# Output stage of a two-layer cross-attention kernel: first operands loaded one stage earlier, layer-norm scaling on ScalarE, head chunks brought in one per tile

## The chip, the cores and the metric

The kernel runs on one core of a Trainium2 chip. The metric is the time of one launch in microseconds (us), lower is better. Before the change three runs gave 2204.09, 2206.16 and 2206.22 us, median 2206.16. The engines are named as the profile names them: PE is TensorE's matmul, PEld its weight load, DVE is VectorE, ACT is ScalarE, POOL is GpSimd and SP is SyncE, which here only issues DMAs. SPq is SP's instruction queue.

## The reference

2048 tokens of width 512 pass through four residual blocks. The last two are computed by the two stages that this document is about:

```python
def _layernorm(x, axis=-1, eps=1e-05):
    m = jnp.mean(x, axis=axis, keepdims=True)
    v = jnp.var(x, axis=axis, keepdims=True)
    return (x - m) / jnp.sqrt(v + eps)

# attention of layer 1, per token over its 16 heads of 32
Q, K, V = (q @ Wq.T + bq), (k @ Wk.T + bk), (v @ Wv.T + bv)      # each reshaped to 16 x 32
attn = softmax(einsum('bshd,bsgd->bshg', Q, K)) ... V
return attn @ Wo.T + bo
# feed-forward of layer 1, weights rounded to -1, 0, 1
w_ternary = jnp.clip(jnp.round(w / mean(abs(w))), -1.0, 1.0)
h = gelu(x @ w1q.T + b1);  return h @ w2q.T + b2
...
x = x + jnp.tanh(g_xattn[1]) * _L1_xattn_ref(_layernorm(x), ctx, ctx, ...)
x = x + jnp.tanh(g_ffn[1]) * _L1_ffn_ref(_layernorm(x), ...)
```

## The kernel before

The program is four stages with a barrier of all engines between them: `l0_attention` (names `a_`), `l0_experts` (`b_`), `l1_attention` (`p_`) and `l1_output_ffn` (`f_`). Each engine's program is written out by hand in order, and engines wait for each other by counting semaphores. Nothing reorders them.

Precision: a matrix product is made of a rounded part ("high") and a remainder ("low") of each operand, so every operand is first copied rounded (ACT) and then subtracted (POOL or DVE). A product of two such operands takes three matmuls (`PASSES`).

`l1_attention` works in 4 blocks of 512 tokens and 8 pairs of units per block (`p` from 0 to 31). Beside it SP brings 32 pieces of the feed-forward weights into the two buffers `w_piece`, and ACT (L1917) and DVE (L2162) sum their magnitudes, one piece each per `p` from `p` = 20 on. A buffer is loaded again (`load_piece`, L1715) when its piece is summed. At the end of each block the heads are stored to `aT` in DRAM (`store_heads`, L1720). The tensor `carry` (16 x 512 per partition) serves as space for weights, queries and context there.

`l1_output_ffn` has two parts. The output part goes over 16 tiles of 128 tokens:

- SP loads the heads as chunks of 128 rows x 512 tokens, four per block of tokens (L2332, ring of 4), the output weights `woT` as four chunks (L2344, two buffers), the bias `bo`, the tokens `x2` (L2346, L2352) and the pieces of the feed-forward weights (L2337).
- ACT rounds each head chunk (L2409) and weight chunk (L2414). POOL makes the low parts of the heads (L2376), DVE those of `woT` (L2519).
- For tile n PE makes the product (`project_out`, L2449, 12 matmuls). DVE adds it to the tokens (L2541) after POOL has added the bias (L2381), takes the statistics (L2544, L2546, L2548), POOL raises variance + eps to the power -0.5 (L2390), and DVE normalises (L2555). PE turns the tile (`turn`, L2458, 4 transposes), ACT rounds the turned tile (L2417) and DVE makes its low part (L2561).
- PE's order is `project_out(n)`, `turn(n - 2)`. DVE's order is add and statistics of n, low part of n - 2, normalise n. ACT rounds two head chunks behind each turned tile for n = 0 to 5, and POOL makes two low parts behind each power (`chunks_beside`).
- Before its first tile DVE rounds two pieces of the feed-forward weights (L2512, L2514).

The second part is the feed-forward over 4 blocks of 512 tokens: `hidden` (L2476, 32 matmuls per group), Gelu on ACT, `down` (L2490, 32 matmuls per group), 4 groups per block. The first `hidden` stands behind the last `turn` on PE.

Of the kernel before, what the change touches and what calls it, by code (L numbers as in the profile page):

```python
# [22 lines left out]
BLK = 512  # L23
# [1453 lines left out]
def l1_attention(nc, new_sem, x_shared, expert_out, place, weight, carry, ctxT, W, w_ffn, x2, qT, kT, vT, aT, sums):  # L1477
# [41 lines left out]
    with ExitStack() as c:  # L1519
# [697 lines left out]
def l1_output_ffn(nc, new_sem, x2, aT, W, w_ffn, sums, out):  # L2217
# [16 lines left out]
    with ExitStack() as c:  # L2234
# [15 lines left out]
        y = sb("y", [P, NT, D])  # L2250
# [29 lines left out]
        w_rounded = sem("w_rounded")  # L2280
        const_in = sem("const_in")
# [3 lines left out]
        x_in = [sem(f"x_in{n}") for n in range(NBLK)]  # L2285
        wo_in = [sem(f"wo_in{s}") for s in range(2)]
# [10 lines left out]
        ln_eps = sem("ln_eps")  # L2297
        ln_rstd = sem("ln_rstd")
# [16 lines left out]
        wo_t = W["woT"].rearrange("(k p) (c n) -> k c p n", p=P, n=BLK)  # L2315
# [372 lines left out]
```

## Time and profile before

| | |
|---|---|
| timed runs, median (range) | 2206.16 us (2204.09 to 2206.22) |
| the profiled execution | 2200.77 us |
| its span, first to last instruction | 2199.0 us |
| PE busy | 1969.6 us, 90% |
| DVE, ACT, POOL busy | 1017.7, 826.7, 1094.9 us |
| mean granted TensorE clock | 0.943 |
| `l1_attention`'s last head copy on ACT ends | 1835.6 us |
| first instruction of `l1_output_ffn` | 1842.4 us |
| first matmul of the feed-forward | 1950.2 us |
| last instruction | 2199.0 us |

The span is read as four stages one behind the other. The output part stands between 1842.4 and 1950.2 us; the rest of the stage is the feed-forward. All times in the rows below are microseconds from the span's start.

### The profile page before, as it was taken

To read this page: it belongs to the slowest core of one execution; us is meant where nothing else is said; L and a number is where in the kernel's file an instruction comes from. 1 tells how busy PE (TensorE), PEld (TensorE's weight loads), DVE (VectorE), ACT (ScalarE), POOL (GpSimd) and SP (SyncE) were. 2 spreads that over 40 slices of the span, in tenths; PEclk is the share of its full clock that TensorE was granted. 3 is DMA by queue.
4 is the path that set the end of the run, shared out by engine and by line. 5 is a ranking of instruction groups with operands and counts; after the bars stand their busy time and mean duration, and the time that the engine had idled before them with its cause. 6 is when DMAs were issued, how large, how long until landed. Compare 5 with 4: busy or idle time off the path is not lost. (4 is left out here: it accounts for less than half of the span.)

```text
span 2199.0 us, 30241 instructions
## 1 busy us (share of the span) xinstructions
PE 1969.6 (90%) x10428; PEld 1649.3 (75%) x10428; DVE 1017.7 (46%) x1561; ACT 826.7 (38%) x1578; POOL 1094.9 (50%) x805
## 2 busy tenths in 40 slices
PE   6999999999999999689996999985799874789998
PEld 5888788878887888478884899983677653568886
DVE  3556654755476547623331333335466343583111
ACT  3336332633363336231211222223377763233332
POOL 6755576557655774441147646606254222533332
PEclk9999999999999999879998999997899966899999
DMA  4232323133313331362326655427676635222000
GB/s 155 82 105 68 116 96 106 53 108 116 107 48 112 101 124 30 118 214 82 139 95 204 197 164 161 131 75 210 175 187 153 169 113 184 81 68 67 19 19 19
DMA packets 173869, 251.29 MB, mean 114 GB/s; under 512 B 45040, under 2 KB 69616, under 8 KB 173744
## 3 DMA queue, kind: packets, MB, share of 16 engines
q1 hardware_dynamic: 158656, 205.23, 30.0%
q0 software_dynamic: 9472, 34.09, 4.9%
q10 hardware_dynamic: 5616, 10.23, 1.2%
q8 instruction: 88, 1.44, 0.3%
q14 instruction: 37, 0.30, 0.0%
HBM read 182.92 MB, written 66.58 MB: 113 GB/s over the span
## 5 line engine op out<-in xcount | busy, mean ns | idle before, releaser
L238 POOL TENSOR_TENSOR a_w_hl<-a_w_raw,a_w_hl 128x2048 fp32r<-128x2048 f32 x65 | 299.8, 4613 | 164.6 <-ACT a_w_hl L300 164.4
L413 PE MATMUL a_proj<-a_c_hl,a_w_hl 128*128 128x512 f32 x768 | 183.2, 399 | 21.4 <-DVE a_w_hl L530 19.6
L300 ACT ACTIVATE a_w_hl<-a_w_raw 128x2048 fp32r<-128x2048 f32 x66 | 126.2, 1912 | 164.6 <-PE a_proj L413 106.7
L413 PEld LDWEIGHTS a_proj<-a_c_hl,a_w_hl 128*128 128x128 f32 x768 | 146.2, 192 | 53.8 <-issue 19.6
L487 PE MATMUL a_proj<-a_w_hl,a_a_hl 128*128 128x512 f32 x768 | 179.5, 392 | 4.0 <-DVE a_a_hl L586 4.0
L413 PE MATMUL a_proj<-a_w_hl,a_c_hl 128*128 128x512 f32 x768 | 181.3, 392 | 0.0
L413 PE MATMUL a_proj<-a_a_hl,a_w_hl 128*128 128x512 f32 x768 | 176.4, 390 | 0.0
L319 ACT ACTIVATE a_sq<-a_proj,a_vecs 128x512 f32<-128x512 f32 x128 | 87.9, 689 | 228.6 <-PE a_proj L413 149.1
L487 PEld LDWEIGHTS a_proj<-a_w_hl,a_a_hl 128*128 128x128 f32 x768 | 142.7, 188 | 34.3 <-POOL a_w_hl L238 5.5
L413 PEld LDWEIGHTS a_proj<-a_a_hl,a_w_hl 128*128 128x128 f32 x768 | 143.6, 188 | 29.7
L262 POOL TENSOR_TENSOR a_ssum<-a_ssum,a_sq 128x512 f32<-128x512 f32 x112 | 145.6, 1300 | 36.9 <-ACT a_sq L319 33.2
L413 PEld LDWEIGHTS a_proj<-a_w_hl,a_c_hl 128*128 128x128 f32 x768 | 142.4, 188 | 28.7
L1252 PE MATMUL b_gate_up<-b_wts,b_xt_hl 128*128 x936 | 159.4, 326 | 4.2 <-DVE b_xt_hl L1451 4.2
L1252 PEld LDWEIGHTS b_gate_up<-b_wts,b_xt_hl 128*128 128x128 f32 x936 | 154.5, 190 | 8.2 <-issue 5.0
L2398 POOL TENSOR_TENSOR f_a_hl<-f_act_sb,f_a_hl 128x512 fp32r<-128x512 f32 x64 | 86.0, 1345 | 149.0 <-ACT f_a_hl L2430 148.9
L1160 PE MATMUL b_gate_up<-b_wts 128*128 128x512 f32 (+1 forms) x576 | 142.0, 407 | 3.0 <-POOL b_wts L937 2.5
L586 DVE SCALAR_TENSOR_TENSOR a_a_hl<-a_qT,a_vecs,a_a_hl 128x512 fp32r<-128x512 f32 x64 | 105.1, 1672 | 83.4 <-ACT a_a_hl L333 83.4
L1160 PEld LDWEIGHTS b_gate_up<-b_wts 128*128 128x128 f32 (+1 forms) x576 | 106.8, 186 | 34.3 <-POOL b_wts L937 2.6
L2490 PE MATMUL f_totals<-f_ternary,f_a_hl 128*128 128x512 f32 x512 | 122.5, 396 | 0.0
L2476 PE MATMUL f_hidden<-f_h_hl,f_ternary 128*128 x512 | 121.0, 394 | 0.0
L1829 POOL TENSOR_TENSOR p_probs<-p_probs,p_rden 128x512 f32<-128x512 f32 x64 | 68.0, 1068 | 99.6 <-DVE p_rden L2158 99.1
L1924 ACT ACTIVATE p_probs<-p_probs,p_mx 128x128 f32<-128x128 f32 x256 | 99.1, 390 | 47.5 <-DVE p_mx L2154 47.4
(245 smaller groups left out, 3682.5 us busy)
## 6 DMA issues: line engine op xcount, KB each, us to landing
a_w_raw<-in_a_ki_w SPq DMA_DIRECT2D x18, 1024.0 KB, 5.2
a_w_raw<-in_a_vi_w SPq DMA_DIRECT2D x16, 1024.0 KB, 5.1
a_w_raw<-in_a_q_w SPq DMA_DIRECT2D x16, 1024.0 KB, 5.1
a_w_raw<-in_a_o_w SPq DMA_DIRECT2D x16, 1024.0 KB, 5.4
b_gu_raw<-in_b_gate_up POOLq DMA_DIRECT2D x32, 352.0 KB, 3.7
l_sorted_rows<-b_zeros SPq DMA_DIRECT2D x39, 256.0 KB, 3.3
b_hs<-l_sorted_rows SPq DMA_DIRECT2D x39, 256.0 KB, 3.2
l_expert_out<-b_yg ACTq DMA_DIRECT2D x39, 256.0 KB, 3.5
```

The costliest lines, as they stand in the source:

```text
L238: pool.tensor_tensor(w_hl[:, s, 1], w_raw[:, s], f32(w_hl[:, s, 0]), ALU.subtract)\
L262: pool.tensor_tensor(ssum[:], first, sq[:, n % 2, :], ALU.add).then_inc(sq_added, 1)
L300: act.activation(w_hl[:, i % 2, 0], w_raw[:, i % 2], ACT.Copy).then_inc(w_high, 1)
L319: act.activation(sq[:, n % 2, :], proj[:, j, :], ACT.Square, bias=bias)\
L413: mm = pe.matmul(proj[:, j, :], left, right, start=(k == 0 and n == 0), stop=(k == KC - 1 and n == 2))
L487: mm = pe.matmul(proj[:, j, :], a_hl[:, ap, k, j * P:(j + 1) * P], w_hl[:, i % 2, wp, k], start=(n == 0 and m == 0), stop=(n == 4 * G - 1 ...
L586: dve.scalar_tensor_tensor(a_hl[:, 1, n % 4, :], qT[:, n, :], v_b[:, n:n + 1], f32(a_hl[:, 0, n % 4, :]), ALU.add, ALU.subtract).then_inc( ...
L1160: mm = pe.matmul(gu_ps[0:w, n, part, :], gu_hl[:, s, wp, k, cols], h_hl[:, hslot, ap, k, :], start=(k == 0 and m == 0), stop=(k == KC - 1 ...
L1252: mm = pe.matmul(gu_ps[:, i % 2, half, 0:F], x_part(i, xp)[:, own], part(r, P, at, F), start=(k == 0 and xp == 0 and start == HI), stop=(k ...
L1924: e = act.activation(probs[:, r, y, :], probs[:, r, y, :], ACT.Exp, bias=mx[:, r, y:y + 1], accum_out=den[:, r, y:y + 1])
L2476: mm = pe.matmul(h_ps[:, m % 2, :], w_t[:, 2 * g, k, f * P:(f + 1) * P], h_hl[:, ap, k, bass.ds(BLK * t, BLK)], start=(k == 0 and ap == 0) ...
L2490: mm = pe.matmul(y_ps[:, j, :], a_hl[:, ap, f, j * P:(j + 1) * P], w_t[:, 2 * g + 1, f, :], start=(m == 0 and ap == 0), stop=(m == NG * FC ...
```

## The change

In `l1_attention`, at `p` = 28, SP issues twelve more loads, of 256 KB each, into `carry`: the four head chunks of the first block of tokens, the four chunks of `woT`, and the first four tiles of tokens. `l1_output_ffn` gets `carry` and uses it as its tile buffer `y`, so these operands lie in place when the stage begins. The tokens of blocks 1 and 3 are loaded where `woT` and the first heads lay, as soon as those are taken.

In the output part, ACT normalises in place of DVE: `Identity` with scale = rstd and bias = -mean x rstd. DVE makes -mean (`neg`), POOL the product (`shift`). Chunks 4 to 7 of the heads are rounded and split before the first tile's power, and from then on one chunk per tile, for n = 0 to 7. The first two pieces of feed-forward weights are rounded by DVE beside tiles 8 and 10, with `act_sb` as their spare buffer, and `tg_b2` is scaled behind the last piece.

```diff
 (l1_attention, SP, in the loop over p)
+                if n == NBLK and w == 4:
+                    sp.wait_ge(c_split, KC * NBLK)
+                    sp.wait_ge(o_out, 16 * NQ)
+                    for k in range(KC):
+                        sp.dma_start(y_next[:, 3 * TPB + k, :], heads_t[k][0]).then_inc(next_in, 16)
+                    sp.wait_ge(s_ready, NP * (NBLK - 1))
+                    for k in range(KC):
+                        sp.dma_start(y_next[:, TPB + k, :], wo_t[k]).then_inc(next_in, 16)
+                    sp.wait_ge(q_moved, NBLK)
+                    for j in range(TPB):
+                        sp.wait_ge(x2_out[j], 16 * NBLK)
+                        sp.dma_start(y_next[:, j, :], x2[j * P:(j + 1) * P, :]).then_inc(next_in, 16)
 (l1_output_ffn)
-        y = sb("y", [P, NT, D])
+        y = carry.rearrange("p (n d) -> p n d", d=D)
+        wo_raw, first_raw = y[:, TPB:2 * TPB, :], y[:, 3 * TPB:4 * TPB, :]
-        def chunks_beside(n):
-            return range(KC + 2 * n, min(KC * NBLK, KC + 2 * n + 2))
+        AHEAD = 2 * KC
+        def chunk_beside(n):
+            return [AHEAD + n] if AHEAD + n < KC * NBLK else []
+        ROUNDED = (8, 10)
 (SP)
-            for k in range(KC):
-                load_chunk(k)
-                if k >= 2:
-                    sp.wait_ge(wo_split, k - 1)
-                sp.dma_start(act_sb[:, k % 2, :], wo_t[k][0]).then_inc(wo_in[k % 2], 16)
-            sp.dma_start(tg_bo[:], W["bo"].to_broadcast([P, D])).then_inc(const_in, 16)
-            sp.dma_start(y[:, 0:TPB, :], x2_t[0]).then_inc(x_in[0], 16)
+            sp.dma_start(tg_bo[:], W["bo"].to_broadcast([P, D])).then_inc(bo_in, 16)
+            for n in range(KC, AHEAD):
+                load_chunk(n)
+            sp.dma_start(y[:, 2 * TPB:3 * TPB, :], x2_t[2]).then_inc(x_in[2], 16)
+            sp.wait_ge(wo_split, KC)
+            sp.dma_start(y[:, TPB:2 * TPB, :], x2_t[1]).then_inc(x_in[1], 16)
+            sp.wait_ge(a_split, KC)
+            sp.dma_start(y[:, 3 * TPB:4 * TPB, :], x2_t[3]).then_inc(x_in[3], 16)
+            for n in range(AHEAD, KC * NBLK):
+                load_chunk(n)
             for m in range(2):
                 load_piece(m)
...
 (POOL)
-            pool.wait_ge(const_done, 2)
+            pool.wait_ge(const_done, 1)
             add_bias(0)
             add_bias(1)
-            for n in range(NT):
-                pool.wait_ge(ln_eps, n + 1)
-                pool.tensor_tensor(rstd[:, n % 2, :], rstd[:, n % 2, :], mhalf[:], ALU.pow).then_inc(ln_rstd, 1)
+            for n in range(KC, AHEAD):
+                a_low(n)
+            for n in range(NT + 2):
+                if n < NT:
+                    pool.wait_ge(ln_eps, 2 * n + 2)
+                    pool.tensor_tensor(rstd[:, n % 2, :], rstd[:, n % 2, :], mhalf[:], ALU.pow).then_inc(ln_pow, 1)
+                    pool.wait_ge(ln_pow, n + 1)
+                    pool.tensor_tensor(shift[:, n % 2, :], neg[:, n % 2, :], rstd[:, n % 2, :], ALU.mult)\
+                        .then_inc(ln_rstd, 1)
                 if n + 2 < NT:
                     add_bias(n + 2)
 (ACT)
+            def normalise(n):
+                s = n % 2
+                act.wait_ge(ln_rstd, n + 1)
+                if n >= 2:
+                    act.wait_ge(h_turned, n - 1)
+                act.activation(hs[:, s, :], y[:, n, :], ACT.Identity, bias=shift[:, s, :], scale=rstd[:, s, :])\
+                    .then_inc(ln_done, 1)
+            for n in range(NT + 2):
+                if n >= 2:
+                    h_high_part(n - 2)
+                if n < NT:
+                    normalise(n)
+                for m in chunk_beside(n):
+                    a_high_part(m)
 (DVE)
-            round_piece(0)
-            round_piece(1)
...
+                if n >= 2:
+                    dve.wait_ge(ln_done, n - 1)
+                dve.tensor_scalar(neg[:, s, :], mv[:, s, 0:1], -1.0, None, ALU.mult).then_inc(ln_eps, 1)
                 dve.tensor_scalar(rstd[:, s, :], mv[:, s, 1:2], LN_EPS, None, ALU.add).then_inc(ln_eps, 1)
...
                 if n >= 2:
                     h_low_part(n - 2)
-                if n < NT:
-                    normalise(n)
+                if n in ROUNDED:
+                    round_piece(ROUNDED.index(n), 0)
```

PE's program is as before. Three places show how the instructions move. The first is SP at the end of `l1_attention` (heads stored to `l_aT`, weight pieces, then the next stage), before:

```order
L1715 DMA p_w_piece<-in_w_ffn 128x512 x12
L1720 DMA l_aT<-p_o 32x16x128 x4
L1715 DMA p_w_piece<-in_w_ffn 128x512 x8
L1720 DMA l_aT<-p_o 32x16x128 x4
L1519 UNCONDITIONAL_BRANCH
L2325 UNCONDITIONAL_BRANCH
L2327 DMA f_gates<-in_d_gates 128x2
```

and after:

```order
L1719 DMA p_w_piece<-in_w_ffn 128x512 x12
L1724 DMA l_aT<-p_o 32x16x128 x4
L1719 DMA p_w_piece<-in_w_ffn 128x512 x2
L1783 DMA carry<-l_aT 128x512 x4
L1786 DMA carry<-in_d_woT 128x512 x4
L1790 DMA carry<-x 128x512 x4
L1719 DMA p_w_piece<-in_w_ffn 128x512 x6
L1724 DMA l_aT<-p_o 32x16x128 x4
L1519 UNCONDITIONAL_BRANCH
L2353 UNCONDITIONAL_BRANCH
L2355 DMA f_gates<-in_d_gates 128x2
```

The twelve loads into `carry` stand between the second and the third of the last eight pieces. The second place is POOL at the start of the output part and over its first tiles (`f_h_hl` is a low part of a head chunk, `f_y` or `carry` the bias added to a tile), before:

```order
L2376 TENSOR_TENSOR f_h_hl<-f_a_raw,f_h_hl 128x512 x4
L2381 TENSOR_TENSOR f_y<-f_y,f_tg_bo 128x512 x2
L2390 TENSOR_TENSOR f_rstd<-f_rstd,f_mhalf 128x1
L2381 TENSOR_TENSOR f_y<-f_y,f_tg_bo 128x512
L2376 TENSOR_TENSOR f_h_hl<-f_a_raw,f_h_hl 128x512 x2
L2390 TENSOR_TENSOR f_rstd<-f_rstd,f_mhalf 128x1
L2381 TENSOR_TENSOR f_y<-f_y,f_tg_bo 128x512
```

and after:

```order
L2403 TENSOR_TENSOR f_h_hl<-carry,f_h_hl 128x512 x4
L2409 TENSOR_TENSOR carry<-carry,f_tg_bo 128x512 x2
L2403 TENSOR_TENSOR f_h_hl<-f_a_raw,f_h_hl 128x512 x4
L2421 TENSOR_TENSOR f_rstd<-f_rstd,f_mhalf 128x1
L2423 TENSOR_TENSOR f_shift<-f_neg,f_rstd 128x1
L2409 TENSOR_TENSOR carry<-carry,f_tg_bo 128x512
L2403 TENSOR_TENSOR f_h_hl<-f_a_raw,f_h_hl 128x512
L2421 TENSOR_TENSOR f_rstd<-f_rstd,f_mhalf 128x1
L2423 TENSOR_TENSOR f_shift<-f_neg,f_rstd 128x1
L2409 TENSOR_TENSOR carry<-carry,f_tg_bo 128x512
L2403 TENSOR_TENSOR f_h_hl<-f_a_raw,f_h_hl 128x512
```

Four more low parts stand ahead of the first power, and each tile then holds power, shift, one bias and one low part. The third place is ACT from the last chunk of weights on (`f_totals` is a turned tile, `f_hs` a normalised one), before:

```order
L2414 ACTIVATE f_a_hl<-f_act_sb 128x512
L2409 ACTIVATE f_h_hl<-f_a_raw 128x512
L2414 ACTIVATE f_a_hl<-f_act_sb 128x512
L2417 ACTIVATE f_h_hl<-f_totals 128x4x128
L2409 ACTIVATE f_h_hl<-f_a_raw 128x512 x2
L2417 ACTIVATE f_h_hl<-f_totals 128x4x128
L2409 ACTIVATE f_h_hl<-f_a_raw 128x512 x2
```

and after:

```order
L2446 ACTIVATE f_a_hl<-carry 128x512
L2461 ACTIVATE f_tgs<-f_gates 128x2
L2442 ACTIVATE f_h_hl<-f_a_raw 128x512 x4
L2452 ACTIVATE f_hs<-carry,f_shift,f_rstd 128x512
L2442 ACTIVATE f_h_hl<-f_a_raw 128x512
L2452 ACTIVATE f_hs<-carry,f_shift,f_rstd 128x512
L2442 ACTIVATE f_h_hl<-f_a_raw 128x512
L2457 ACTIVATE f_h_hl<-f_totals 128x4x128
L2452 ACTIVATE f_hs<-carry,f_shift,f_rstd 128x512
L2442 ACTIVATE f_h_hl<-f_a_raw 128x512
L2457 ACTIVATE f_h_hl<-f_totals 128x4x128
```

The normalising of tile n stands between the copy of the turned tile n - 2 and one chunk.

## Rows read from the trace of the kernel before

**Rows 1.** Chain of waits, start of the stage: start us, us, what.
```profile
1842.80 0.42 SPq L2332
...
1844.21 4.33 DMA f_act_sb<-in_d_woT
...
1852.18 8.40 DMA f_w_raw<-in_w_ffn
...
1865.94 1.27 POOL f_y L2381
```
**Rows 2.** Chain of waits, one tile with two chunks.
```profile
1904.59 2.52 POOL f_h_hl L2376 x2
1907.11 0.52 POOL f_rstd L2390
...
1907.66 1.48 DVE f_hs L2555
...
1909.18 0.67 PE f_totals L2458 x4
```
**Rows 3.** Timeline, a tile without chunks: start us, us, engine, line [idle before <-releaser].
```profile
1923.46 0.74 DVE L2541 SCALAR_TENSOR_TENSOR f_y<-f_totals,f_tgs,f_y 128x512 f32<-128x512 f32 x1
...
1925.18 0.15 DVE L2548 TENSOR_SCALAR f_rstd<-f_mv 128x1 f32<-128x1 f32 x1
1925.25 0.68 DVE L2561 TENSOR_TENSOR f_h_hl<-f_totals,f_h_hl 128x512 fp32r<-128x512 f32 x1
...
1926.00 1.51 DVE L2555 TENSOR_SCALAR f_hs<-f_y,f_mv,f_rstd 128x512 f32<-128x512 f32 x1
```
**Rows 4.** Timeline, first turn, last projection, a late normalising, first feed-forward matmuls.
```profile
1873.15 0.60 PE L2458 MATMUL f_totals<-f_ident,f_hs 128*128 128x128 f32 x4
...
1940.22 3.05 PE L2449 MATMUL f_totals<-f_a_hl,f_h_hl 128*128 128x512 f32 x12
...
1945.84 0.55 DVE L2555 TENSOR_SCALAR f_hs<-f_y,f_mv,f_rstd 128x512 f32<-128x512 f32 x1
...
1950.21 6.04 PE L2476 MATMUL f_hidden<-f_h_hl,f_ternary 128*128 x16
```
**Rows 5.** Timeline, POOL's first low parts.
```profile
1847.33 4.63 POOL L2376 TENSOR_TENSOR f_h_hl<-f_a_raw,f_h_hl 128x512 fp32r<-128x512 f32 x3
```
**Rows 6.** Timeline, an Identity with a bias on ACT.
```profile
1700.37 0.68 ACT L1888 ACTIVATE p_outs<-p_proj,p_bias 128x512 f32<-128x512 f32 x1
```
**Rows 7.** Timeline, a short DVE operation beside two long ones of POOL.
```profile
1497.51 3.00 POOL L1823 TENSOR_TENSOR p_w_hl<-carry,p_w_hl 128x512 fp32r<-128x512 f32 x2
...
1499.07 0.15 DVE L2112 TENSOR_SCALAR p_rstd<-p_mv 128x1 f32<-128x1 f32 x1
```
**Rows 8.** Chain of waits, one group of the feed-forward.
```profile
1967.39 7.25 PE f_hidden L2476 x32
```
**Rows 9.** Timeline, a weight piece rounded alone and one beside POOL.
```profile
1952.48 0.75 DVE L2512 TENSOR_SCALAR f_hs<-f_w_raw,f_thr 128x1024 f32<-128x1024 f32 x1 [0.57 <-DVE f_h_hl L2561]
1953.27 1.28 DVE L2514 SCALAR_TENSOR_TENSOR f_ternary<-f_w_raw,f_thr,f_hs 128x1024 fp32r<-128x1024 f32 x1
...
1988.11 1.60 DVE L2512 TENSOR_SCALAR f_hs<-f_w_raw,f_thr 128x1024 f32<-128x1024 f32 x1
1989.74 2.20 DVE L2514 SCALAR_TENSOR_TENSOR f_ternary<-f_w_raw,f_thr,f_hs 128x1024 fp32r<-128x1024 f32 x1
```
**Rows 10.** Timeline, end of `l1_attention`: SP's pieces and DVE's sums.
```profile
1805.07 21.81 SPq L1715 DMA_DIRECT2D p_w_piece<-in_w_ffn  x8
...
1815.75 0.66 DVE L2162 TENSOR_REDUCE magnitudes<-p_w_piece 128x1 f32<-128x512 f32 x1
...
1819.37 0.69 DVE L2150 TENSOR_TENSOR p_probs<-p_scores,p_mask 128x512 f32<-128x512 f32 x1 [2.96 <-PE p_scores L2043]
```
**Rows 11.** Stretches: us, PE, PEld, DVE, ACT, POOL busy, PEclk, DMA share, GB/s.
```profile
1848.00:1855.00 7.00, 4.94 (x9) 2.50 (x9) 3.87 (x4) 3.68 (x6) 5.03 (x4) 0.50 0.72 203
1855.00:1868.00 13.00, 5.30 (x15) 3.92 (x15) 6.75 (x11) 0.00 (x0) 2.25 (x3) 0.76 1.00 368
```

More of the change, by code:

```diff
@@ L1473, in _, with l1_attention @@
                     take_tile(i - 2)
-def l1_attention(nc, new_sem, x_shared, expert_out, place, weight, carry, ctxT, W, w_ffn, x2, qT, kT, vT, aT, sums):
+def l1_attention(nc, new_sem, x_shared, expert_out, place, weight, carry, ctxT, W, w_ffn, woT, x2, qT, kT, vT, aT, sums):
     T, D = x2.shape
@@ L1609, in l1_attention @@
         o_out = sem("o_out")
+        next_in = sem("next_in")
+        y_next = carry.rearrange("p (n d) -> p n d", d=D)
+        heads_t = aT.rearrange("(k p) (b t) -> k b p t", p=P, t=BLK)
+        wo_t = woT.rearrange("(k p) n -> k p n", p=P)
         x_t, x2_t = (a.rearrange("(b n p) d -> n b p d", p=P, n=TPB) for a in (x_shared, x2))
@@ L2214, in _, with l1_output_ffn @@
             reciprocal(2 * NP * NBLK - 1)
-def l1_output_ffn(nc, new_sem, x2, aT, W, w_ffn, sums, out):
+def l1_output_ffn(nc, new_sem, x2, aT, W, w_ffn, sums, carry, out):
     T, D = x2.shape
@@ L2270, in l1_output_ffn @@
         rstd = sb("rstd", [P, 2, 1])
-        w_neg = hs[:].rearrange("p s d -> p (s d)")
+        neg = sb("neg", [P, 2, 1])
+        shift = sb("shift", [P, 2, 1])
+        w_neg = {0: act_sb[:].rearrange("p s d -> p (s d)"), 1: hs[:].rearrange("p s d -> p (s d)")}
         gates_in = sem("gates_in")
@@ L2284, in l1_output_ffn @@
         const_done = sem("const_done")
-        x_in = [sem(f"x_in{n}") for n in range(NBLK)]
-        wo_in = [sem(f"wo_in{s}") for s in range(2)]
+        x_in = {n: sem(f"x_in{n}") for n in range(1, NBLK)}
         wo_high = sem("wo_high")
@@ L2297, in l1_output_ffn @@
         ln_eps = sem("ln_eps")
+        ln_pow = sem("ln_pow")
         ln_rstd = sem("ln_rstd")
@@ L2418, in _ @@
                                y_ps[:, 2 + n % 2, :].rearrange("p (k n) -> p k n", k=KC), ACT.Copy).then_inc(h_high, 1)
-                for m in chunks_beside(n):
+            act.wait_ge(gates_in, 16)
+            act.activation(tgs[:], gates[:], ACT.Tanh).then_inc(tg_ready, 1)
+            for n in range(KC, AHEAD):
+                a_high_part(n)
+            for n in range(NT + 2):
[3 more added lines that the diff above has]
+                    normalise(n)
+                for m in chunk_beside(n):
                     a_high_part(m)
-            act.wait_ge(const_in, 48)
+            act.wait_ge(const_in, 32)
             with act.Fori(0, NBLK) as t:
@@ L2629, in build @@
                 stage(l1_attention, x_shared, expert_out, place, weight, carry[:], a["ctxT"], part("c_"), a["w_ffn"],
-                      x2, qT, kT, vT, aT, sums)
-            stage(l1_output_ffn, x2, aT, part("d_"), a["w_ffn"], sums, out)
+                      a["d_woT"], x2, qT, kT, vT, aT, sums)
+                stage(l1_output_ffn, x2, aT, part("d_"), a["w_ffn"], sums, carry[:], out)
     last[0].close()
```

59 lines of the change are left out of this document (25 added, 34 removed).

## The prediction

> **What bounds the kernel now.** I read the chain of waits first, from its end back. The feed-forward is PE without a gap, one group of 32 matmuls after the other in 7.25 us [rows 8], from the first `hidden` matmul at 1950.21 us on. So everything that the change can bring is an earlier start of that matmul; the work behind it keeps its order, and I take it as unchanged.
>
> The part before it splits in three on the chain. At the start the chain is loads and their users: a weight chunk takes 4.33 us from issue to landing, then the stage waits 8.40 us for a weight piece, because DVE rounds two pieces before it scales the bias, and POOL adds the first bias only at 1865.94 [rows 1]. PE turns tile 0 at 1873.15 [rows 4]. In the tiles with two chunks the chain goes through POOL and DVE: two low parts 2.52, power 0.52, normalising 1.48, turn 0.67, from 1904.59 to 1909.85 [rows 2], and then ACT's copy of the turned tile and of the next chunk, 0.6 each, before POOL can go on: 6.5 us per tile. In the tiles without chunks DVE is full: from the add at 1923.46 to the end of the normalising at 1927.5 (1926.00 + 1.51) it does one tile in 4.0 us, of which normalising takes 1.51 [rows 3]. The same instruction takes 0.55 where POOL adds no bias beside it [rows 4].
>
> **The change, part by part.** All times are on the clock of the profiled execution (2200.77 us, span 2199.0).
>
> *Start up to the first turn.* The heads, `woT` and tokens lie in place. ACT needs 8 copies of some 0.65 us [rows 6], from 1842.4 to about 1847.6, so it is early. POOL starts no earlier than before: its first low part began at 1847.33 [rows 5], behind its own constants and the clearing of semaphores, which stays. From there POOL is the queue: four low parts at 1.3 (between 1.26 [rows 2] and 1.54, that is 4.63 / 3 [rows 5]) to 1852.6, two biases at 1.27 [rows 1] to 1855.2, four low parts at 1.26 to 1860.2, power 0.55 to 1860.8. The new product `shift` is not in the trace. It is a POOL operation on 128x1 like the power, so at most 0.57; it can't be less than nothing; I take 0.5 and 0.1 for the wait between the two, to 1861.4. The normalising on ACT: an Identity with a bias on 128x512 took 0.68 [rows 6]; I take 0.7, with 0.5 and 1.0 as ends, to 1862.1. PE has done tiles 0 to 2 by then, at the low clock at first (granted 0.50, which is 1.2 GHz, in 1848 to 1855, behind a wait of 12 us) [rows 11]. First turn: 1862.1 instead of 1873.15, 11 us saved. The tokens' loads go with it at no cost: they are asked for by POOL's second tile at the earliest.
>
> *Tiles with a chunk (n = 0 to 7).* Per tile POOL does power 0.52, shift 0.6, bias 1.27, low part 1.26 = 3.65 us. The chunk's copy stands on ACT behind the normalising: shift ends at 1.1, normalising at 1.85, copy at 2.5, low part at 3.75. I take 3.75 per tile, the cover being nearly gone: every 0.1 us more on ACT's normalising is 0.1 more per tile. Turn 8 then comes at 1862.1 + 8 x 3.75 = 1892.1.
>
> *What PE can do.* Its tile is 12 matmuls and 4 transposes. In the feed-forward, where nothing is waited for, a matmul of this width takes 7.25 / 32 = 0.227 us [rows 8], so 12 take 2.72, plus about 0.45 for the turn: 3.17. The bound on the other side is the 3.05 that 12 matmuls show alone [rows 4] plus the turn's 0.67 and a gap, 3.8. I take 3.2, since `project_out(n)` waits only for the add of n - 2 and the turn for a tile two behind. DVE without the normalising: 1923.46 to 1925.93 is 2.47, plus 0.08 for `neg`, 2.6 [rows 3].
>
> *Tiles 8 to 15.* Four more turns at 3.2 bring 1904.9, then project 15 starts 0.45 later and takes 3.05: 1908.4. Beside them DVE rounds two pieces. One takes 0.75 + 1.28 alone and 1.60 + 2.20 beside POOL [rows 9]; at 3 us each, DVE has 4 x 2.6 + 6 = 16.4 us for four tiles in which PE has 12.8, and the two-tile lead on PE gives back most of it. I put 1.5 on the path (0 to 4). Project 15 ends at 1909.9 instead of 1943.27 (1940.22 + 3.05).
>
> *Tail.* Before, DVE lagged and 6.94 us passed from 1943.27 to 1950.21. Now: add, statistics, mean and variance 2.0 (1923.46 to 1925.33, plus `neg` and a semaphore), power 0.6, shift 0.6, normalising 0.75, turn 0.75 = 4.7. The feed-forward starts at 1914.6, 35.6 us earlier.
>
> *The twelve loads in `l1_attention`.* SP sends them between 1806 and 1812 (0.47 us each with the gap [rows 1]), where it had been idle till ACT's next sum, so the issue is covered. Their 3.1 MB are not: DMA moved 368 GB/s at full share, and 203 at 0.72 share with chunks, that is 280 [rows 11]. So they drain in 8.5 to 11 us, to 1817 or 1819, and the two pieces behind them land at 1818 to 1820.5. DVE sums one at 1815.75 and then has 2.96 us of idle time up to 1819.37 [rows 10]. The stall is 0 to 2 us; I take 1.5, and 5 as the outer end, if the next pair is late as well. The Trainium skill ("DMA: Bandwidth & Descriptors", Queues, rings and completion order) says that the DMAs of one issuing engine run on one row of rings and are consumed in ring order. By that rule the pieces can't overtake the loads, as I have assumed from the 8.40 us of a 512 KB piece behind a 1 MB load; if they could, this term would be 0.
>
> *Edits at nothing.* `tg_b2` scaled behind the last piece (DVE is done with the pieces long before the first `down` ends), the waits on `next_in` (landed by 1820, asked for at 1842), one more semaphore. ACT's switch between Copy, Identity and Tanh: in `l1_attention` Identity stands between Exps and copies with no table load in the rows, and the program has one load in this stage, before Gelu, as before.
>
> **The sum.** 35.6 - 1.5 = 34.1 us. Profiled execution 2200.77 - 34.1 = 2166.7. The timed median was 2206.16, 5.4 above the profiled one, so the forecast is 2172 us timed.
>
> **A rule that speaks against it.** `neg` and `rstd` are single-source operations on DVE and now fall beside POOL's long operations. In the trace a 128x1 operation of that kind took 0.15 us in the middle of two POOL operations that lasted 3.00 [rows 7], while the 128x512 one took 1.51 against 0.55 [rows 3, 4]. The Trainium skill ("GPSIMD Engine Reference", Key points) says that GpSimd shares its SBUF interfaces with VectorE and contends with its instructions in a two-port mode or with two SBUF inputs. The normalising agrees with it; read strictly it would hold the two short ones as well, which rows 7 doesn't show. By the rule so read, the time would be that of rival 1.
>
> **The rivals.**
> 1. *The short operations on DVE wait out POOL's.* Two of them per tile at up to 1.27 each: DVE 2.6 + 2.5 = 5.1 per tile. Turn 13 at 1862.1 + 13 x 5.1 = 1928.4, feed-forward at about 1935: saved 15 - 1.5 = 13.5, timed 2192.5. For: the normalising did so. Against: rows 7. Chance 0.04.
> 2. *The start isn't shortened*, because a first copy or POOL's low parts are held by something that the loads had hidden so far (ACT's first instruction, the bias landing late). Price up to 11 us: timed 2183. For: SP's first chunk load leaves at 1842.80 [rows 1], and no row shows what ACT and POOL do when nothing is awaited from it. Against: nothing that the first copies need is loaded in the stage any more. Chance 0.06.
> 3. *POOL or ACT is slower per tile than reckoned and PE takes 3.8*: normalising 1.0 on ACT, or stretched low parts. 4.1 x 8 for the first tiles (2.8 more), 0.6 x 4 for the others (2.4), rounding hidden in it (-1.5): some 4 to 5 us, timed 2176. It lies in the range. Chance 0.14.
> 4. *Slower than before: the tiles run in lockstep.* ACT's order puts the copy of turned tile n - 2 ahead of normalising n, and DVE's waits on `ln_done` stand ahead of its low part; if one of them closes a loop over one tile, its length is project 3.05 + DVE 2.0 + power and shift 1.2 + normalising 0.7 + turn 0.7 + copy 0.6 + low part 0.7 = 8.9 us. Turn 15 would be at 1862.1 + 15 x 8.9 = 1995.6, 46 us behind the old one: timed some 2253. It becomes slower than before from 5.8 us per tile ((1949.4 - 1862.1) / 15). For: every buffer is only two deep. Against: with the same depths the old kernel ran at 4.0 [rows 3], and the loop that I find (turn, copy, normalising) is 2 us long over two tiles. Chance 0.02.
> That the change doesn't do what it says, for example that the loads land in `carry` too late, is excluded by 20 us between their landing and the barrier.
>
> **How the numbers follow.** Forecast 0.74, rival 1 0.04, rival 2 0.06, rival 3 0.14, rival 4 0.02. The forecast's own ends: rounding and stall both hidden, 3 us better, 2169, and shift, normalising and DMA cheaper, 2166; on the other side the stall at 5 and the rounding at 4 make 2178. With rival 3 and the reach towards rival 2 the range is 2163 to 2184. A difference under 0.2% (4.4 us) can't be told from no change. Only rival 4 is slower: faster 0.97, same 0.01, slower 0.02.
>
> **What would show it.** First turn near 1862 and first low part of POOL still near 1847.4 (plus the stall); turns 3.7 to 3.8 apart up to turn 8, with POOL or ACT's normalising named as what ended PE's waits; about 3.2 apart behind that, with DVE named at tiles 9 to 12; 4.7 us from the last projection to the first `hidden`; the first DVE sum behind the twelve loads 2 to 5 us late and the last head copy 0 to 2 us late; the granted clock at 1.00 from turn 0 on. The forecast is wrong if turns stay over 4.5 apart, if `neg` takes over 0.5 us, or if the feed-forward itself becomes longer than 2199.0 - 1950.2 = 248.8 us by more than 1.

## The result and the profile after

The changed kernel took 2168.32 us (median of four, 2160.28 to 2171.64) against 2205.12 us for the kernel before beside it. The ratio is 0.9837, 95% interval 0.9806 to 0.9867. The forecast was 2172 us. A second comparison, beside the last experiments, gave 2167.29 us and 0.9834 (0.9811 to 0.9857). The profiled execution took 2160.28 us with a span of 2158.5.

| from the stage's first instruction | before | after | forecast |
|---|---|---|---|
| first turn of a tile | 30.75 | 19.45 | 19.7 |
| turn 8 | 81.20 | 48.70 | 49.7 |
| last projection ends | 100.87 | 66.04 | 67.5 |
| first `hidden` | 107.81 | 70.45 | 72.2 |
| first `down` | 117.33 | 78.33 | |
| last instruction | 356.60 | 317.67 | 321.0 |

The stage begins at 1842.40 us before and at 1840.83 after.

The chain of waits through the first tile and one steady tile of the changed kernel (start us, us, what; POOLq is POOL's sequencer, L2662 clears a semaphore):

```profile
1840.85 0.04 POOLq L2662
...
1845.23 0.20 POOL f_ones L2392
...
1845.97 5.13 POOL f_h_hl L2403 x4
1851.10 2.50 POOL carry L2409 x2
1853.60 4.98 POOL f_h_hl L2403 x4
1858.58 0.54 POOL f_rstd L2421
...
1859.19 0.20 POOL f_shift L2423
...
1859.41 0.81 ACT f_hs L2452
...
1866.21 0.20 POOL f_shift L2423
...
1867.15 0.62 ACT f_h_hl L2442
...
1867.85 1.29 POOL f_h_hl L2403
1869.13 0.52 POOL f_rstd L2421
```

No DMA stands on it any more [rows 1 had two]. For 4.4 us the chain is POOL clearing semaphores, and from 1845.97 on 12.6 us of POOL's low parts and biases without a gap, then power, shift and ACT's normalising. The steady tile is the loop that the prediction described: shift 1866.21, normalising 0.81, the chunk's copy 1867.15, low part 1867.85, power 1869.13, and the next shift 3.51 us behind the first. In [rows 2] it was 6.5. PE is behind this loop at first: turn 1 comes 4.85 us behind turn 0. Turns 1 to 6 are then 3.23 to 3.27 us apart, and at turn 7 PE has caught up with the loop. So turn 7 stands 24.6 us behind turn 0, seven times 3.51.

The timeline around tiles 8 and 10, where a weight piece is rounded:

```profile
1886.45 0.80 DVE L2562 TENSOR_SCALAR f_act_sb<-f_w_raw,f_thr 128x1024 f32<-128x1024 f32 x1
1886.66 1.00 POOL L2421 TENSOR_TENSOR f_rstd<-f_rstd,f_mhalf 128x1 f32<-128x1 f32 x1
1887.29 1.28 DVE L2564 SCALAR_TENSOR_TENSOR f_ternary<-f_w_raw,f_thr,f_act_sb 128x1024 fp32r<-128x1024 f32 x1
1887.74 0.88 POOL L2423 TENSOR_TENSOR f_shift<-f_neg,f_rstd 128x1 f32<-128x1 f32 x1
...
1888.66 0.81 ACT L2452 ACTIVATE f_hs<-carry,f_shift,f_rstd 128x512 f32<-128x512 f32 x1 [2.84 <-POOL f_shift L2423]
...
1889.53 0.66 PE L2508 MATMUL f_totals<-f_ident,f_hs 128*128 128x128 f32 x4 [1.20 <-ACT f_hs L2452]
...
1897.33 3.05 PE L2499 MATMUL f_totals<-f_a_hl,f_h_hl 128*128 128x512 f32 x12 [0.65 <-DVE carry L2587]
```

At tile 8 DVE isn't late. POOL is: its power takes 1.00 us instead of 0.55 and its shift 0.88 instead of 0.20, both beside a rounding operation, and PE waits 1.20 us for the normalising behind them. Behind tile 10 PE waits 0.65 us for DVE itself (its add of tile 11), and turn 11 comes 0.9 us late.

The timeline of the tail, and DVE behind it:

```profile
1906.98 0.75 DVE L2587 SCALAR_TENSOR_TENSOR carry<-f_totals,f_tgs,carry 128x512 f32<-128x512 f32 x1 [0.66 <-PE f_totals L2499]
...
1909.01 0.55 POOL L2421 TENSOR_TENSOR f_rstd<-f_rstd,f_mhalf 128x1 f32<-128x1 f32 x1 [2.39 <-DVE f_rstd L2597]
...
1910.72 0.66 PE L2508 MATMUL f_totals<-f_ident,f_hs 128*128 128x128 f32 x4 [2.55 <-ACT f_hs L2452]
...
1911.28 7.53 PE L2526 MATMUL f_hidden<-f_h_hl,f_ternary 128*128 x32
...
1919.16 2.13 PE L2540 MATMUL f_totals<-f_ternary,f_a_hl 128*128 128x512 f32 x8 [0.35 <-DVE f_ternary L2564]
```

The last add starts as soon as the last projection ends, so DVE has no arrears. From the last projection's end to the first `hidden` it is 4.4 us, where it was 6.94 before [rows 4]. And the timeline at the end of `l1_attention`, which answers to [rows 10]:

```profile
1806.34 2.34 SPq L1790 DMA_DIRECT2D carry<-x  x4
...
1808.72 8.58 SPq L1719 DMA_DIRECT2D p_w_piece<-in_w_ffn  x4
...
1813.70 1.21 PE L2060 MATMUL p_scores<-p_k,carry 32*128 32x128 f32 x16
1815.67 0.63 ACT L1934 ACTIVATE p_w_piece<-p_w_piece 128x512 f32<-128x512 f32 x1 [1.94 <-DMA p_w_piece<-in_w_ffn]
...
1816.26 0.69 DVE L2179 TENSOR_REDUCE magnitudes<-p_w_piece 128x1 f32<-128x512 f32 x1 [4.82 <-DMA p_w_piece<-in_w_ffn]
1816.87 0.68 DVE L2167 TENSOR_TENSOR p_probs<-p_scores,p_mask 128x512 f32<-128x512 f32 x1
...
1822.42 2.08 PE L2060 MATMUL p_scores<-p_k,carry 32*128 32x128 f32 x16
```

Both sums wait for pieces issued from 1808.72 on, behind the twelve loads. The twelve have landed by 1815.0 and the two pieces at 1815.65 and 1816.24. That is 6.9 and 7.0 us behind their issue, and the next pair needs 2.8. DVE's masking stands behind its sum, and the score groups, 6.83 to 6.88 us apart just ahead of this, are 8.72 apart here. Behind this gap PE's next score group takes 2.08 us instead of 1.21, at a lower clock (granted 0.50 from 1817.3 to 1830.9). From the fourth last score group to the next stage it is 40.78 us, and 38.00 before: the stall costs 2.8 us, once.

### The profile page after: what moved, and what is told of

Its sections match the earlier page's. It is cut to its first block and busy times, and to the rows that moved or that the text cites. A ratio compares the mean times of both kernels' runs of the same rounds, so it can differ in the third digit from the quotient of the medians.

```text
span 2158.5 us, 30291 instructions
## 1 busy us (share of the span) xinstructions
PE 1953.0 (90%) x10428; PEld 1641.9 (76%) x10428; DVE 998.5 (46%) x1561; ACT 837.7 (39%) x1594; POOL 1099.1 (51%) x821
```

## The experiments

In twelve runs the stage of the output began anywhere from 1836.1 to 1849.6 us of the span, with the same code ahead of it but for the loads. `l1_attention` itself began at 1478.5 to 1488.9. That spread is larger than most effects looked for, so I read each variant from its trace, by spans inside the stage, and give the timed ratio beside it. "Attention's end" is the time from the fourth last score group to the first instruction of the output stage.

| | attention's end | first turn | first `hidden` | stage | timed, ratio to before |
|---|---|---|---|---|---|
| before | 38.00 | 30.75 | 107.81 | 356.60 | |
| after | 40.78 | 19.45 | 70.45 | 317.67 | 0.9837 |
| x9 after again | 40.73 | 19.44 | 70.49 | 317.69 | 0.9834 |
| x1 loads late | 37.99 | 23.12 | 76.20 | 324.30 | 0.9876 |
| x2 rounding first | 40.60 | 23.05 | 71.93 | 320.14 | 0.9863 |
| x3 DVE normalises | 40.36 | 21.06 | 83.36 | 331.21 | 0.9904 |
| x4 two chunks | 40.24 | 17.18 | 73.74 | 321.37 | 0.9861 |
| x5 before, ACT normalises | 37.98 | 30.96 | 84.73 | 333.04 | 0.9879 |
| x6 loads spread | 37.97 | 19.43 | 70.41 | 318.59 | 0.9817 |
| x7 copy first | 40.30 | 19.89 | 68.52 | 316.70 | 0.9821 |
| x8 start as before | 38.01 | 29.17 | 78.16 | 326.92 | 0.9853 |
| x10 start balanced | 37.99 | 19.84 | 68.32 | 316.42 | 0.9822 |
| x11 spread and copy | 37.97 | 19.75 | 68.76 | 316.59 | 0.9823 |
| x12 behind the pieces | 40.71 | 19.47 | 70.49 | 317.69 | one run |

The first column has two values and nothing between: 37.97 to 38.01 without the burst of twelve loads, 40.24 to 40.78 with it.

### x3 and x5: what the normalising on ScalarE is worth

```diff
 x3, the changed kernel
-                if n < NT:
-                    normalise(n)        (ACT)
+                if n < NT:
+                    normalise(n)        (DVE, behind h_low_part; no neg, no shift)
```

> The changed kernel, but DVE normalises as before; no neg and no shift. Theory A (DVE becomes the bound): 3.9 us per tile instead of 3.5 and 3.25, the rounding of two pieces fully on the path (+4), tail +2: 13 to 17 us slower than the changed kernel, about 2182. Theory B (PE and POOL bound the tiles, the move of the normalising is worth little): 3 us slower.

Measured: first `hidden` 12.9 us later, stage 13.5 us longer, 2180.30 us, ratio 0.9904 (0.9872 to 0.9936). Theory A holds in size and place: the turns are 3.97 us apart, and the tail takes 6.94 us instead of 4.4. DVE in x3, one tile:

```profile
1882.78 1.51 DVE L2588 TENSOR_SCALAR f_hs<-carry,f_mv,f_rstd 128x512 f32<-128x512 f32 x1
1884.21 0.74 DVE L2574 SCALAR_TENSOR_TENSOR carry<-f_totals,f_tgs,carry 128x512 f32<-128x512 f32 x1
...
1886.75 1.51 DVE L2588 TENSOR_SCALAR f_hs<-carry,f_mv,f_rstd 128x512 f32<-128x512 f32 x1
```

The period is 3.97 us and DVE is never idle in it.

```diff
 x5, the kernel before
+ DVE:  neg = -mean;  POOL: shift = neg * rstd behind the power
+ ACT:  h_high_part(n - 2), normalise(n), chunks_beside(n)
- DVE:  normalise(n)
```

> The kernel before, with one part of the change alone: ScalarE normalises, with neg on DVE and shift on POOL. Loads, chunks and rounding as before. Theory A (DVE's normalising set the period in both kinds of tile; with two chunks POOL then takes the 4.8 us that x4_two_chunks showed): first turn still at 30.7 us behind the stage's start, 1.7 us less for each of some 6 tiles, 0.75 less for 8, 4 less at the tail: 17 to 21 us faster than before, some 2185. Theory B (the parts add up, so this one is worth what its undoing cost, 13.5 us): 2190.

Measured: 2179.38 us, ratio 0.9879 (0.9849 to 0.9909); first `hidden` at 84.73 instead of 107.81, so 23.1 us earlier from this part alone. Both theories were too small. Between turns 2 and 6 they are 4.06 us apart on average (6.5 before); only two intervals reach the 4.8 of POOL's loop with two chunks, in the others PE uses up the lead that POOL had. And 6.0 us are won ahead of turn 2 (47.28 before, 41.25 in x5), which I had not counted at all. So this part is worth 23.1 us when it is added first (x5) and 12.9 when it is taken away last (x3): what a part is worth depends on which others stand.

### x1, x2 and x8: what the start is made of

```diff
 x1: no loads into carry in l1_attention; in the output stage
+            for k in range(KC):
+                sp.dma_start(first_raw[:, k, :], a_t[k][0]).then_inc(op_in[2 * k], 16)
+                sp.dma_start(wo_raw[:, k, :], wo_t[k]).then_inc(op_in[2 * k + 1], 16)
 x2: in DVE's program ahead of tg_bo (SP loads both pieces behind bo)
+            round_piece(0, 0)
+            round_piece(1, 0)
 x8: both
```

> The changed kernel, but the twelve operands are loaded at the start of the output stage (heads and weights by turns, then bias and tokens), none in the attention stage. Theory A (POOL and DVE's rounding set the old start, the loads only a part): POOL starts its low parts about 5 us behind the stage's start as now, the biases wait for the tokens to 14.5 to 17.5, the second four low parts follow, first turn at 22 to 27 us instead of 19.45; the stall of 1.9 us in the attention stage goes. Net 1 to 5 us slower than the changed kernel, 2169 to 2174 timed. Theory B (the loads a stage ahead carry the 11 us of the start): first turn at 30 us, 9 us slower, about 2177.

> The changed kernel, but the first two weight pieces are rounded ahead of tile 0 as before the change (SP loads them behind the output bias), and tg_bo is scaled behind them. Theory A (either the rounding or the late loads alone would have held the start, so one of them costs little): rounding lies beside POOL's first four low parts, bias from 11.2 us behind the stage's start instead of 10.2, and the 1.20 and 0.65 us that PE waits beside tiles 8 and 10 go; within 2 us of the changed kernel. Theory B (moving the rounding is what shortened the start): 6 us or more slower.

> The changed kernel with both changes of the start undone: operands loaded in the output stage, and two weight pieces rounded ahead of tile 0. Either alone gave the first turn at 23.1 us behind the stage's start (19.45 with neither). Theory A (they stand one behind the other: the pieces queue behind the operands and the biases behind the rounding): first turn at 30 to 33 us, so 7 to 10 more than either alone. Theory B (they overlap): 24 to 26 us.

Measured: first turn at 23.1 us with either undone, at 29.2 with both, and at 19.45 with neither. In x1 POOL's bias waits 2.60 us for the tokens, in x2 2.35 us for DVE behind the rounding, in x8:

```profile
1855.96 0.75 DVE L2557 TENSOR_SCALAR f_act_sb<-f_w_raw,f_thr 128x1024 f32<-128x1024 f32 x1 [2.81 <-DMA f_w_raw<-in_w_ffn]
...
1860.14 0.48 DVE L2577 TENSOR_SCALAR f_tg_bo<-f_tg_bo,f_tgs 128x512 f32<-128x512 f32 x1
```

So of the 9.7 us at the start the part made first wins 6.1 and the second 3.6, whichever is which. In x1 the first turn lies in theory A's 22 to 27. The first `hidden` is 5.8 us late, 2.1 of them behind the first turn: turns 1 to 7 are all 3.52 apart, at the pace of POOL's loop, where PE in the changed kernel caught up with it. Less the 2.8 us of the stall that x1 avoids, and with a slower first `hidden` group, the trace is 3.8 us worse than that of the changed kernel, within theory A's 1 to 5; the timed median, 2174.27, lies 0.3 outside its range. x2 holds to theory A in the total and not at the start: its first turn is 3.6 us late, and the first `hidden` only 1.5, since nothing waits beside tiles 8 and 10. From the first turn on x2 is 2.1 us faster than the changed kernel, which is what the rounding costs there. x8's first turn is just outside theory A's 30 to 33.

### x4: one chunk per tile or two

```diff
-            return [AHEAD + n] if AHEAD + n < KC * NBLK else []
+            return list(range(KC + 2 * n, min(KC * NBLK, KC + 2 * n + 2)))
```

> The changed kernel, but no chunks ahead of the first power and two per tile beside tiles 0 to 5, as before the change. Theory A (POOL has to make the same low parts either way, and PE has its three projections done only at 17 us): turns from 17.2 us on, 4.9 us apart for six tiles, turn 8 at 51 to 53 us instead of 48.7: 2 to 4.5 us slower. Theory B (the period of the old tiles, 6.5 us, comes from the two chunks): 3 us per tile, 18 us slower.

Measured: first turn 17.18, first `hidden` 3.3 us later, ratio 0.9861 (0.9825 to 0.9897). Theory A holds in the total (2 to 4.5 us) and less well in the turns. POOL's powers are 4.7 to 4.8 us apart, as it said, but the turns are that far apart only twice. Between turns 1 and 2 it is 7.34 us: `project_out(4)` waits 2.43 us for POOL's low part and then takes 4.46 us, at a granted clock of 0.64. Turn 8 comes at 50.7, just ahead of theory A's 51 to 53. From x5 (two chunks, old start) to x8 (one chunk, old start) it is 6.6 us, so this part too is worth more in the other order.

### x6 and x12: the stall in `l1_attention`

```diff
 x12: the block of twelve loads, word for word, moved from ahead of
      load_piece to behind it in the same pair of units
 x6:  the same place, four loads at w == 4, four at w == 5, four at w == 6
```

> The changed kernel, with the twelve early loads spread over three pairs of units, four behind the weight pieces of each, in place of all twelve between two pieces. Theory A (the stall is pieces queued behind 3.1 MB of loads): all intervals between score groups 6.8 to 6.9 us, 0.9 to 1.9 us gained ahead of the output stage, the output stage as in the changed kernel. Theory B (the stall comes from the sum of bytes in the memory or in the engines, wherever they are issued): the interval of 7.7 to 8.7 us stays or splits into several of 7.3.

> The changed kernel with all twelve loads in one burst, moved behind the two weight pieces of the same pair of units (x6 did that and spread them). Theory A (what is late is a piece queued behind the burst; the next piece is now issued some 6 us later, when 2 of the 8.5 to 11 us of draining are left, and is needed 6.8 us after that): no interval over 6.9 us. Theory B (the burst itself disturbs whatever runs beside it): an interval of 7.7 to 8.7 us remains.

x6: attention's end takes 37.97 us, as before the change, and the output stage up to the first `hidden` is the same within 0.04 us; 2164.30 us, ratio 0.9817 (0.9788 to 0.9845). Theory A, with 2.8 us gained where it had put 0.9 to 1.9.

x12: the last seven intervals between score groups are 6.83 to 6.89 us, as theory A had it, but attention's end takes 40.71. My measure was too narrow: the stall had moved behind the last score group. SP, ACT and DVE in x12 there, and DVE's sum in x6:

```profile
1821.94 2.35 SPq L1807 DMA_DIRECT2D carry<-x  x4
...
1824.33 9.38 SPq L1719 DMA_DIRECT2D p_w_piece<-in_w_ffn  x4
...
1832.15 0.63 ACT L1934 ACTIVATE p_w_piece<-p_w_piece 128x512 f32<-128x512 f32 x1 [2.30 <-DMA p_w_piece<-in_w_ffn]
...
1832.62 0.69 DVE L2179 TENSOR_REDUCE magnitudes<-p_w_piece 128x1 f32<-128x512 f32 x1 [5.53 <-DMA p_w_piece<-in_w_ffn]
```

```profile
1829.46 0.66 DVE L2181 TENSOR_REDUCE magnitudes<-p_w_piece 128x1 f32<-128x512 f32 x1
```

The pieces of the next pair are issued at 1824.33, right behind the last of the twelve loads, and land 7.8 us later, so they are as late as those in the changed kernel. The stall comes wherever in the pair the burst stands: a burst of twelve drains longer than the gap to the next piece (its last load lands 5.7 us behind the issue of that piece). With bursts of four it is 1.1 us at most, and the piece lands 2.7 us behind its issue, as usual. In every trace with the burst of twelve the first piece behind it lands only when the last of the twelve has landed, which speaks for a queue in order. That agrees with the Trainium skill ("DMA: Bandwidth & Descriptors", Queues, rings and completion order), by which the DMAs of one issuing engine are consumed in ring order. No run put the loads on another engine's queue, so that contention for the memory has a part in it isn't excluded.

### x7: the order of ACT's copy and normalising

```diff
-                if n < NT:
-                    normalise(n)
                 for m in chunk_beside(n):
                     a_high_part(m)
+                if n < NT:
+                    normalise(n)
```

> The changed kernel, with ACT's copy of the next head chunk ahead of the normalising instead of behind it. Theory A (the 3.51 us per tile of the first eight is shift, normalising, copy, low part and power one behind the other): POOL's own work, 3.4 us, becomes the period, and the normalising waits at most for the rest of a copy: 0.05 to 0.2 us less per tile, about 1 us less for the output part. Theory B (POOL itself is the bound at 3.51): no change. Theory C (the copy now delays the normalising): up to 0.6 us more per tile, 5 us slower.

Measured: all turns from 1 to 10 are 3.24 to 3.28 apart, PE waits at tile 8 no more, and the first `hidden` is 1.9 us earlier; ratio 0.9821 (0.9787 to 0.9855). Theory A holds in direction: with the copy out of the loop POOL's powers come 3.27 us apart, where they were 3.51. But up to turn 7 this wins nothing on PE. Its first turn is 0.4 us later, and turn 7 stands at 44.17, where it stood at 44.04. The gain lies behind that, in the lead that POOL and ACT now have over PE:

```profile
1888.33 0.88 POOL L2423 TENSOR_TENSOR f_shift<-f_neg,f_rstd 128x1 f32<-128x1 f32 x1
...
1889.25 0.82 ACT L2452 ACTIVATE f_hs<-carry,f_shift,f_rstd 128x512 f32<-128x512 f32 x1 [3.13 <-POOL f_shift L2423]
...
1890.77 0.60 PE L2508 MATMUL f_totals<-f_ident,f_hs 128*128 128x128 f32 x4
```

The shift of tile 8 is as slow as before (0.88), but the normalising ends 0.7 us ahead of its turn, and PE doesn't wait. That is 1.3 us at turn 8, and 0.6 more at turn 11.

### x9 to x11: the changed kernel again, and two attempts at a better one

```diff
 x10, over x6 and x7:
+ DVE: low parts of head chunks 0 to 3, between those of the weights
+ PE:  project_out(0) ahead of the matmul of the means
+ POOL: of chunks 4 to 7 two low parts ahead of the first power (four before), low part ahead of the bias in each tile
+ DVE: the two halves of a rounding beside tiles 9, 10 and 11, 12
```

> The changed kernel once more, beside the two that follow. Ratio to before 0.984 within its interval. In the trace: first turn 19.4 to 19.9 us behind the stage's start, first hidden at 70.4; theory A (the first hidden group at full clock, 7.53 us, in the first profile was a matter of that one run, since three variants with the same work ahead of it had 9.1): the first hidden group takes 8.5 to 9.2 us and the stage 318.5 us in place of 317.7. Theory B (it is a lasting gain of the change): 7.5 us. One interval of the last score groups is 0.9 to 1.9 us longer than 6.84.

> The changed kernel with the loads spread behind the pieces, the chunk copied ahead of the normalising, and more: DVE makes the low parts of the first four head chunks, PE projects tile 0 ahead of the matmul of the means (so it doesn't wait for POOL's constants), POOL makes two low parts ahead of the first power instead of four and puts each tile's low part ahead of its bias, and DVE rounds the two pieces in halves beside tiles 9 to 12. Theory A (POOL's queue of 4.4 us of cleared semaphores and 17 us of work was the start's bound): first turn at 14 to 16 us instead of 19.45, turns 3.3 to 3.45 apart up to turn 9, first hidden at 61 to 65 us instead of 70.4; 7 to 10 us faster than the changed kernel with the stall gone. Theory B (PE's cold first projections are the bound): first turn at 17 to 18 us, 3 to 5 us faster.

> The changed kernel with x6 and x7 together: loads spread behind the pieces and the chunk's copy ahead of the normalising. Theory A (the two are in different stages and add up): no long score interval, first hidden at 68.5 us; 0.9 to 1.9 + 1.9 = 2.8 to 3.8 us faster than the changed kernel, about 2163 to 2165 timed. Theory B (one of them was the noise of a single trace): 1 to 2 us.

x9: theory A fell. The first `hidden` group takes 7.53 us again, as in x12; the last section has more on it.

x10: neither theory. POOL's queue was ended early as meant, and shift of tile 0 was done at 1855.45, 11.9 us behind the stage's start instead of 18.6. But ACT's in-order copy of chunk 8 then stood ahead of the normalising and waited for its DMA:

```profile
1849.14 0.39 SPq L2382 DMA_DIRECT2D carry<-x  x1
1849.58 0.74 SPq L2384 DMA_DIRECT2D carry<-x  x1
1853.43 6.82 SPq L2369 DMA_DIRECT2D f_a_raw<-l_aT  x4
...
1861.98 0.63 ACT L2449 ACTIVATE f_h_hl<-f_a_raw 128x512 fp32r<-128x512 f32 x1 [7.37 <-DMA f_a_raw<-l_aT]
1862.51 0.80 ACT L2459 ACTIVATE f_hs<-carry,f_shift,f_rstd 128x512 f32<-128x512 f32 x1
...
1863.37 1.12 PE L2511 MATMUL f_totals<-f_ident,f_hs 128*128 128x128 f32 x4 [6.88 <-ACT f_hs L2459]
```

The chunk is asked for at 1853.43, when its buffer is free, and lands 8.5 us later, behind the 2 MB of tokens issued at 1849.14 and 1849.58, the last of which land at 1861.3. PE waited 6.88 us and the granted clock fell with it, to 0.50 from 1860.3 to 1867.2. What the start won was all given back there. From turn 1 to turn 13 they are 3.24 apart, and nothing waits beside tiles 8 and 10, so the halved rounding is hidden. The obvious next step, chunks 8 and 9 loaded ahead of the tokens of blocks 1 and 3, wasn't tried.

x11: 2163.74 us against 2167.29 for the changed kernel beside it; ratios 0.9823 (0.9806 to 0.9839) and 0.9834 (0.9811 to 0.9857). In the traces it gains 1.7 us up to the first `hidden` and the stall of 2.8, and gives back 0.6 behind the first `hidden`: 3.9, where the medians differ by 3.6. The intervals of the timed ratios overlap, so that x11 is the better kernel rests on its traces.

## Why the prediction was right

*Start*: 11.0 us forecast, 11.30 measured. POOL was the queue as described (first low part at 1845.97, 5.1 us behind the stage's start). The share of the twelve loads was worked out nowhere and is smaller than the text suggests: 3.7 us by x1, if the rounding is out of the way.

*Shift and normalising*: 0.20 against 0.5, and 0.81 against 0.7 (the Identity with two operands per partition is 0.13 longer than in [rows 6]). The errors nearly cancel. POOL's loop was 3.51 instead of 3.75, and turns 0 to 8 took 29.25 us instead of 30.0. That this came so near is in part luck. The sign that was named, turns 3.7 to 3.8 apart with POOL or ACT ending PE's waits, did not show: the loop gives 8 x 3.51 = 28.1 us, and the other 1.1 are the wait at tile 8, which the prediction had in another term. That "every 0.1 us more on ACT's normalising is 0.1 more per tile" holds turn by turn only where PE rides on the loop, as in x1 and x8, at 3.52. In the changed kernel PE was itself catching up until turn 7.

*Tiles on PE*: 3.2 forecast, 3.23 to 3.27 measured. PE finished projections 0 to 2 before the first turn, but "the granted clock at 1.00 from turn 0 on" was wrong:

```profile
1860.00:1889.00 29.00, 28.00 (x128) 22.03 (x128) 19.64 (x45) 13.81 (x24) 26.71 (x33) 0.94 0.29 90
1889.00:1907.00 18.00, 16.82 (x83) 13.53 (x84) 16.68 (x39) 7.79 (x13) 11.90 (x18) 1.00 0.18 59
```

The columns are those of [rows 11]. Behind its wait of 2.35 us the granted clock was 0.50 from 1861.6 to 1865.0, and PE did `project_out(3)` in 4.60 us instead of 3.05. The end hardly saw it, since PE then caught up with POOL's loop.

*Rounding*: 1.5 forecast, waits of 1.20 + 0.65 = 1.85 measured, and 2.1 in all by the comparison with x2. More than half of it comes in a way that the prediction did not have: not through DVE's time, but through POOL's power and shift stretched beside it. x7 removes the first wait though DVE rounds at the same tile and POOL is as slow, because the normalising has a lead over PE there.

*Tail*: 4.7 forecast, 1911.28 - 1906.87 = 4.4 measured. The feed-forward starts 37.4 us earlier within the stage instead of 35.6.

*Stall*: 1.5 forecast, with 5 as the outer end; 2.8 and 2.7 measured (40.78 and 40.73 less 38.0). 1.9 of it is the late sum, in the way described: it is 4.82 us late, and 2.96 of that was idle time before. The whole end of `l1_attention` ahead of the stall lies 4.4 us earlier than in the trace of before. With that set off, SP issued the loads at 1806.2 to 1812.5, where 1806 to 1812 was forecast, and the pieces landed at 1820.0 and 1820.6, where it was 1818 to 1820.5. The other 0.9 is the slower score group behind the gap, which the prediction did not have.

*Feed-forward unchanged*: 247.2 us instead of 248.8 from the first `hidden` on. This step was wrong by 1.6. The first group took 7.53 us where it had taken 9.69, since the clock stayed up in the tail (it was granted 0.50 in 1950 to 1953 before), and 0.5 of that is lost before the first `down`, where PE now waits 0.35 us for DVE's rounding. About 1.0 of the 1.6 is luck: x6 has the same code in this stage, and there the clock fell and the feed-forward took 248.2 us.

*The sum*: 37.4 + 1.6 - 2.8 = 36.2 us is what the traces assign to the change; the timed medians give 36.8. The profiled execution came out at 2160.28, 6.4 below the forecast of 2166.7: 1.8 from the output part, 1.6 from the feed-forward, and 3.1 from the stage starting at 1840.83 instead of 1843.9. With the stall at 2.8, the code ahead of it must have taken 4.4 us less than in the trace of before. `l1_attention` began 2.3 us later than before (1483.79 against 1481.47), so within it 6.7 us were won, which the change does not explain and x9, the same kernel, doesn't repeat (its stage begins at 1847.79). Over all traces `l1_attention` took 357.0 to 363.6 us; why is open.

*Rivals*: 1 (short DVE operations wait for POOL) did not occur; `neg` takes 0.15 us and `rstd` 0.14 in all 16 tiles. 2 (the start isn't shortened) did not. 3 (POOL or ACT slower per tile) no: 3.51 and 3.24. 4 (lockstep) no. Which part did the most: in the order before, x5, x8, after, the normalising brings the first `hidden` 23.1 us forward, the chunks 6.6 (x5 to x8, which also differ in where the operands lie) and the start 7.7.

## What to carry to other kernels

Look for the loop between engines before moving work: here an operation of 1.5 us on VectorE stood in a loop with two of GpSimd's and with PE's next tile, and moving it to the idle ScalarE was worth more than all loads and buffers, in either order in which the parts were tried. In the order of an in-order engine an operation that waits for a DMA belongs behind the one that the critical loop waits for, unless the data is sure to be there (x7 against x10). A prefetch in the queue of a running loop goes out in portions that drain before the loop's next transfer is needed (x6); moving the whole burst only moves the stall (x12).

## What the hardware showed that I had not expected

- *GpSimd is stretched by VectorE too, even at one element per partition.* Beside DVE's rounding of 128x1024, POOL's power on 128x1 took 1.00 us instead of 0.55 and the product 0.88 instead of 0.20, ending within 0.05 us of DVE's operation (1887.74 + 0.88 = 1888.62, 1887.29 + 1.28 = 1888.57). In x2 the four first low parts took 6.39 us beside the rounding instead of 5.13. The other way round, DVE's 128x1 operations stayed at 0.15, but a 128x2 one took 0.56 in the changed kernel at the start and 1.16 in x10:

```profile
1851.02 1.16 DVE L2590 TENSOR_SCALAR f_thr<-f_mean 128x2 f32<-128x2 f32 x1
1852.10 0.15 DVE L2591 TENSOR_SCALAR f_thr<-f_mean 128x2 f32<-128x2 f32 x1
```

  It ends where POOL's bias additions end (1849.63 + 2.52 = 1852.15). So a short operation of DVE can be as long as the rest of a long one of POOL, and rival 1 was less remote than its 0.04. The operations that showed it are on 128x2 and those in the tiles on 128x1; no run tells whether that makes the difference.
- *The clock behind the same gap came out in two ways.* Ahead of the last turn PE waits 2.54 to 2.58 us in every variant where ACT normalises, x10 excepted. In the changed kernel, x9 and x12 the granted clock stayed at 1.00 and the group took 7.53 us. In x6, x7 and x11 it fell to 0.50, which is 1.2 GHz, and the group took 8.8 to 9.1; in the others it took 8.5 to 9.2. Stretches of x7:

```profile
1909.00:1911.00 2.00, 0.00 (x0) 0.00 (x0) 1.05 (x5) 0.55 (x1) 0.74 (x2) 1.00 0.00 0
1911.00:1913.00 2.00, 1.68 (x8) 1.39 (x9) 1.05 (x2) 1.72 (x4) 0.00 (x0) 0.87 0.00 0
1913.00:1915.00 2.00, 2.00 (x7) 1.54 (x6) 1.75 (x3) 0.91 (x1) 0.00 (x0) 0.50 0.05 12
```

  Here the fall comes 1.2 us behind the end of PE's wait (1911.32), when it is busy again; in the other traces with ACT normalising in which it fell, the fall lies between 0.6 us ahead of that end (x1) and 1.5 behind it (x6). x6 differs from the changed kernel in nothing of this stage, so the work alone doesn't decide it.
- *Clearing semaphores takes 0.07 us each on POOL.* 64 of them stand at the head of the stage, 4.4 us, while the other engines already work; before the change this lay under the loads' latency.
